# Segment sum of every eighth edge tile as two products of rounded parts, and lane one-hots compared with an iota in PSUM

## The reference

```python
def _L0_gnn_ref(node_features, edge_index, edge_features, mW1, mb1, ...):
    node_i = node_features[i_idx]
    node_j = node_features[j_idx]
    msg_input = jnp.concatenate([node_i, node_j, edge_features], axis=-1)
    h = jax.nn.relu(msg_input @ mW1 + mb1)
    messages = h @ mW2 + mb2
    aggregated = jax.ops.segment_sum(messages, i_idx, num_segments=node_features.shape[0])
    ...
```

## Time and profile before

| | us |
|---|---|
| median of 3 runs | 2928.23 |
| the runs | 2925.83, 2928.23, 2932.85 |
| the profiled execution | 2927.9 |
| its span, first to last instruction | 2926.1 |

### The profile page before, as it was taken

The page is one execution under the profiler, slowest core; times in us unless marked ns, Lnnn a source line. Parts: engine busy times, 40 slices in busy tenths (PEclk is TensorE's granted clock), DMA queues, the critical chain, the costliest instruction groups (busy, mean ns, idle before and its releaser), DMA issues. The chain is left out here.

```text
span 2926.1 us, 34808 instructions
## 1 busy us (share of the span) xinstructions
PE 2337.2 (80%) x8554; PEld 1421.9 (49%) x8554; DVE 1870.9 (64%) x3838; ACT 1030.2 (35%) x2853; POOL 1804.0 (62%) x1842
## 2 busy tenths in 40 slices
PE   5488898229999999998998887888876655556799
PEld 2144443115555555555666664555454433334577
DVE  8897785217777777774544456666645444444898
ACT  1177878217677777662222221000030000000232
POOL 5777777777677676761006566777747777777200
PEclk8799999559999999999999999999778788888899
DMA  9223225029999999996016565555344333333001
GB/s 282 75 62 105 85 87 173 14 65 271 261 270 267 262 266 265 265 264 211 28 56 207 160 200 173 167 169 168 104 124 124 105 106 105 106 105 106 19 1 45
DMA packets 229078, 433.58 MB, mean 148 GB/s; under 512 B 45882, under 2 KB 121292, under 8 KB 228686
## 3 DMA queue, kind: packets, MB, share of 16 engines
q0 software_dynamic: 93888, 248.27, 31.7%
q1 hardware_dynamic: 129504, 177.80, 18.4%
q10 hardware_dynamic: 5488, 5.28, 0.5%
HBM read 310.36 MB, written 122.99 MB: 148 GB/s over the span
## 5 line engine op out<-in xcount | busy, mean ns | idle before, releaser
L958 POOL DMA_INDIRECT qg<-q_d,rb x480 | 479.0, 998 | 207.3 <-issue 103.5
L419 POOL DMA_INDIRECT recs_d<-recs,slot_src x416 | 451.8, 1086 | 146.1 <-issue 132.3
L1909 POOL DMA_INDIRECT nbr_yg<-y_d,gidx x439 | 415.2, 946 | 156.7 <-issue 86.8
L1075 PE MATMUL p_sum<-hb,wide 128*96 128x512 f32 x960 | 451.9, 593 | 1.2 <-ACT hb L1004 1.1
L1004 ACT ACTIVATE hb<-hb 128x512 f32<-128x512 f32 x480 | 297.1, 630 | 205.2 <-DVE hb L1044 201.2
L1748 POOL DMA_INDIRECT nbr_yg<-y_d,gidx x298 | 282.4, 948 | 94.4 <-issue 57.6
L1044 DVE TENSOR_TENSOR hb<-p_h,qg 128x512 f32<-128x512 f32 x480 | 312.6, 680 | 35.3 <-DMA qg<-q_d,rb 31.4
L1349 POOL DMA_INDIRECT n_ahead<-y_d,gidx x141 | 134.8, 956 | 268.8 <-DMA y_d<-n_y 198.5
L443 ACT ACTIVATE lane_hot<-bare_hot,val 128x128 f16<-128x128 f16 x832 | 247.5, 391 | 130.4 <-DVE bare_hot L729 130.1
L1845 PE MATMUL nbr_sum<-nbr_yg,nbr_hot 128*128 128x258 f32 x596 | 215.9, 460 | 67.8 <-DMA nbr_yg<-y_d,gidx 55.8
L1030 DVE SCALAR_TENSOR_TENSOR agg<-agg,keep,p_sum 96x512 f32<-96x512 f32 x240 | 178.1, 742 | 123.3 <-PE p_sum L1075 122.4
(11 more groups left out here) (377 smaller groups left out, 4084.6 us busy)
## 6 DMA issues: line engine op xcount, KB each, us to landing
agg_d<-agg SPq DMA_DIRECT2D x240, 192.4 KB, 5.0
msg_d<-n_ahead SPq DMA_DIRECT2D x141, 128.0 KB, 2.7
nbr_ys<-msg_d SPq DMA_DIRECT2D x141, 128.0 KB, 2.7
nbr_yg<-y_d,gidx POOLq DMA_INDIRECT x737, 2.8
p_low<-p_d SPq DMA_DIRECT2D x11, 768.0 KB, 12.5
recs_d<-fill SPq DMA_DIRECT2D x16, 510.0 KB, 17.5
rb<-recs_d SPq DMA_DIRECT2D x60, 136.0 KB, 5.1
qg<-q_d,rb POOLq DMA_INDIRECT x480, 5.7
```

The source lines that it names most:

```text
L419: pool.indirect_dma_start(S.recs[:, :], bass.IndirectOffsetOnAxis(ap=slot_src[:, c:c + 1], axis=0), recs[:, c, :], None).then_inc(s_scat, 16)
L958: pool.indirect_dma_start(qg[t % QB][:, :], None, S.q[:, :], bass.IndirectOffsetOnAxis(ap=rb[n % RB][:, t % BT, 1:2].bitcast(U32), axis=0) ...
L1075: last = pe.matmul(p_sum[g % 2][0:SB, :], wide[g % XB][:, j, 0:SB], hb[t % HB][:, :], start=(j == 0), stop=(j == 1))
L1909: pool.indirect_dma_start(yg[t % GB][:, 0:D], None, S.y[0:EARLY_NODES, :] if t < NSTORED else S.y[:, :], bass.IndirectOffsetOnAxis(ap=C.gi ...
```

## The change

The lane one-hots: the first 64 numbers of the iota are copied once to `p_iota[:, 440:504]` in PSUM (`lane_row`). Line 729 becomes two instructions, one for each half of the 128 lanes, which add 0 or 64 to `lane_row` and compare with the lane number.

The segment sum: for tiles 0, 8, 16, ... (`is_split`, 60 of 480) ACT writes relu rounded into `h_high` in place of `hb`. A new DVE instruction (`low_part`, behind both additions of the pair) computes max(hb, 0) - h_high into `h_low`. PE multiplies the one-hot part of `wide` with `h_high` and then with `h_low`, both as products of rounded operands, in place of one f32 product. `wide` has the type fp32r now; where it is used in f32 it is only read as such. ACT and DVE wait for the sums of the split tile two before (`s_sum`), PE for `s_h_low`.

The semaphore of the last stage's stores is allocated in `build`.

```diff
@@ sorting_programs
+        lane_row = p_iota[:, NCOL:NCOL + P // 2]
...
             step.link(dve.tensor_copy(iota_c[:, :], lo_i[:, :]))
+            step.link(dve.tensor_copy(lane_row, C.iota_f[:, 0:P // 2]))
...
-            lane_iota = C.iota_f[:, :].rearrange("p (a n) -> p a n", a=1)
+            lane_iota = lane_row.rearrange("p (a n) -> p a n", a=1)
...
-                dve.tensor_tensor(bare_hot[g % BARE][:, :, :], lane_iota.to_broadcast([P, TC, P]),
-                                  lane[:, TC * g:TC * g + TC].rearrange("p (c a) -> p c a", a=1).to_broadcast([P, TC, P]),
-                                  ALU.is_equal).then_inc(s_bare, 1)
+                for half in range(2):
+                    last = dve.scalar_tensor_tensor(
+                        out=bare_hot[g % BARE][:, :, half * P // 2:(half + 1) * P // 2],
+                        in0=lane_iota.to_broadcast([P, TC, P // 2]), scalar=float(half * P // 2),
+                        in1=lane[:, TC * g:TC * g + TC].rearrange("p (c a) -> p c a", a=1).to_broadcast([P, TC, P // 2]),
+                        op0=ALU.add, op1=ALU.is_equal)
+                last.then_inc(s_bare, 1)
@@ stage_sort_and_edges
-        LOAD = 4
+        LOAD, EACH_SPLIT = 4, 4
...
-        wide = [m.sb(f"wide{b}", [P, 2, P]) for b in range(XB)]
+        wide = [m.sb(f"wide{b}", [P, 2, P], F32R) for b in range(XB)]
...
+        h_high = [m.sb(f"h_high{b}", [P, HID], F32R) for b in range(2)]
+        h_low = [m.sb(f"h_low{b}", [P, HID], F32R) for b in range(2)]
...
+        def is_split(t):
+            return t % (2 * EACH_SPLIT) == 0
...
-                        act.activation(hb[t % HB][:, :], hb[t % HB][:, :], ACT.Relu).then_inc(s_relu, 1)
+                        into = hb[t % HB]
+                        if is_split(t):
+                            n = g // EACH_SPLIT
+                            if n >= 2:
+                                act.wait_ge(s_sum, EACH_SPLIT * (n - 2) + 1)
+                            into = h_high[n % 2]
+                        act.activation(into[:, :], hb[t % HB][:, :], ACT.Relu).then_inc(s_relu, 1)
...
+                def low_part(t):
+                    dve.wait_ge(s_relu, t + 1)
+                    n = t // (2 * EACH_SPLIT)
+                    if n >= 2:
+                        dve.wait_ge(s_sum, EACH_SPLIT * (n - 2) + 1)
+                    dve.scalar_tensor_tensor(out=h_low[t // (2 * EACH_SPLIT) % 2][:, :], in0=hb[t % HB][:, :], scalar=0.0,
+                                             in1=h_high[t // (2 * EACH_SPLIT) % 2][:, :].bitcast(F32), op0=ALU.max,
+                                             op1=ALU.subtract).then_inc(s_h_low, 1)
...
+                    if is_split(2 * g):
+                        low_part(2 * g)
...
-                        last = pe.matmul(p_sum[g % 2][0:SB, :], wide[g % XB][:, j, 0:SB], hb[t % HB][:, :],
-                                         start=(j == 0), stop=(j == 1))
+                        if is_split(t):
+                            hot = wide[g % XB][:, j, 0:SB]
+                            pe.matmul(p_sum[g % 2][0:SB, :], hot, h_high[t // (2 * EACH_SPLIT) % 2][:, :], start=(j == 0), stop=False)
+                            pe.wait_ge(s_h_low, t // (2 * EACH_SPLIT) + 1)
+                            last = pe.matmul(p_sum[g % 2][0:SB, :], hot, h_low[t // (2 * EACH_SPLIT) % 2][:, :], start=False, stop=(j == 1))
+                        else:
+                            last = pe.matmul(p_sum[g % 2][0:SB, :], wide[g % XB][:, j, 0:SB].bitcast(F32), hb[t % HB][:, :],
+                                             start=(j == 0), stop=(j == 1))
```

More of the change, by code:

```diff
@@ L899, in stage_sort_and_edges @@
         s_first, s_acc, s_deg = m.sem("e_first"), m.sem("e_acc"), m.sem("e_deg")
+        s_h_low = m.sem("e_h_low")
         recs_v = S.recs[0:NSLOTS, :].rearrange("(n p r) w -> n p r w", p=P, r=BT)
@@ L1053, in transposes @@
                     for j in range(2):
-                        last = pe.transpose(p_tr[g % 2][:, j, :], wide[g % XB][:, j, :], C.ident[:, :])
+                        last = pe.transpose(p_tr[g % 2][:, j, :], wide[g % XB][:, j, :].bitcast(F32), C.ident[:, :])
                     last.then_inc(s_tr, 1)
@@ L2075, in stage_last @@
         s_x3, s_ln, s_weigh, s_sum = (m.sem(n) for n in ("x3", "ln", "weigh", "sum"))
-        s_route, s_dve, s_z, s_out, s_st = (m.sem(n) for n in ("route", "dve", "z", "out_done", "st"))
+        s_route, s_dve, s_z, s_out = (m.sem(n) for n in ("route", "dve", "z", "out_done"))
+        s_st = C.s_out_stored
         FIRST_TURN, FIRST_SPREAD = (0, 3, 10, 19, 22), (6, 8, 13, 15, 17)
@@ L2272, in build @@
         S.msg = dram("msg_d", [NSTORED * P, D])
+        C.s_out_stored = m.sem("out_stored")
         stage_constants(nc, C)
```

## The result

The changed kernel takes 2885.0 us (median of 4 runs, 2879.1 to 2888.6), the kernel before beside it 2930.1: a ratio of 0.9845 with a 95% interval of 0.9824 to 0.9867, so 45 us or 1.5% faster. The forecast was 2871 with a range of 2856 to 2894: right in direction and inside the range, 14 us too hopeful. The number alone does not part it from the rivals: A and D gave 2888, E 2881 to 2891. What parts them is in the traces. The profiled execution took 2885.8 us, its span is 2884.0.

The account below looks back on a forecast made before the run. POOL's 416 scatters were taken to bound the first 640 us and PE the edge stage. Terms: 2927.9 - 41.4 + 0.2 + 0.5 - 16.5 = 2870.7, against the median 2871 us; range 2856 to 2894.

Parts of the forecast that it names:

- A: Rival, edge stage: gathers become its bound, so it gives nothing; 2888 us, chance 0.10.
- D: Rival, edge stage: low part at half rate, 1.22 us, holds POOL 1.06 us, no edge gain; 2888 us, chance 0.03.
- E: Rival, sort stage: scatter gain partly lost waiting for the placing, 10 to 20 us; 2881 to 2891 us, chance 0.05.
- What bounds each stage: First 640 us end with POOL's list of 416 scatters; in the edge stage PE is busy 690.67 of 692 us.
- The hold by two tensors in SBUF: Sort stage: DVE instructions with both tensors in SBUF stretch POOL's scatters; iota in PSUM frees 41.4 us.
- B: Rival, sort stage: new halves hold POOL too, 8 us more stretch, edge saving kept; 2920 us, chance 0.06.
- C: Rival, both stages: every scalar_tensor_tensor holds POOL and gathers bound the edge stage; 2973 us at most, chance 0.02.
- the rule of 0.87 us for each us of DVE work: POOL's hold by DVE instructions with two SBUF tensors; up to 0.6 us for each low part.
- What is late next in the sort stage: Scatters also wait for the placing; these waits were to grow by 0.5 us, 3 us as the worst.
- DVE's cost of the halves: Sort stage: two halves take 1.39 us against 1.22, 9 us on DVE, covered by idle time before the edge stage.
- The split products: Edge stage, 60 split tiles: two rounded products cost PE 0.48 us instead of 0.855; low part 693 ns.
- Their worth: Edge stage: 22.5 us saved on PE, of which 16.5 us was taken as arriving because gathers are late next.

Follow-up runs that it names:

- e3: Changed kernel with the iota of the one-hot halves read from SBUF instead of PSUM; 3311 us (one run) beside 3285 for the kernel before, slower chip.
- e5: Changed kernel with split tiles' sum written back to PSUM, where relu and low part read it; 2877.9 us, ratio 0.9820.
- e1: Kernel before with the change of the lane one-hots alone; 3299.1 us beside 3285.4 on a slower chip, ratio 1.0024.
- e8: Changed kernel with scatters allowed four more groups ahead of the placing (PLACE_LAG 14 instead of 10); 2877.3 us, ratio 0.9817.
- e6: Changed kernel with eight gather buffers (qg) instead of six; 2872.1 us, ratio 0.9805.

## Why the prediction was right or wrong

**What bounds each stage: right where the kernel before takes 2930 us.** POOL's list ended the sort stage and PE's products filled the edge stage; taking from both shortened both.

**The hold by two tensors in SBUF: right in cause and size.** The stretch expected to go was 41.4 us, and POOL's busy time in scatters fell by 41.3. e3 shows that the place of the iota decides whether there is a hold. So B (the halves hold POOL too) and C (every scalar_tensor_tensor does) are out, the latter also by e5's 0.94 us. What the prediction had wrong is the rule of 0.87 us for each us of DVE work, which its rivals B, C and D are priced with: it holds for a scatter that starts with the DVE instruction. One that starts before it is not held, and one that starts late in it is held for the rest alone. The forecast of 41.4 us did not use the rule, it took the whole stretch away. It also gave PSUM all the credit, where on the chip of e1 to e3 a third of it comes from the halving.

**What is late next in the sort stage: the step that failed.** I had 0.5 us for longer waits for the placing, 3 as the worst; it was 2.6 at scatter 76 in the profiled execution, for a reason that I had not added up: the scatters ahead of it came 3 us sooner, while the first lane one-hot started 1 us later in this execution (137.94 against 136.87). With an earlier start, as in e5, this wait is not there, so it belongs to the execution as much as to the change. And 5.9 us went into pauses before every 113th scatter, which I had not seen as pauses: in the earlier trace rows they hide in the "issue" time. These pauses grew in all five executions of the faster scatters outside the slower chips, by 4.5 to 6.7 us in all. Idle time of a list that bounds a stage has to be taken apart by size before the list is made faster, not taken as a mean of 0.3 us. This term was 8 to 9 us too good. The 0.2 us for the copy of the iota can't be seen: the first lane one-hot starts at 136.4 to 137.9 us with the copy, at 136.9 without.

**DVE's cost of the halves: right, on the safe side.** The pair takes 1.28 us, less than two times 0.69, and the idle time before the edge stage covered it.

**The split products: right on PE** (0.47 us for two), on the low part's time (0.69 us, so no halved rate, and D is out) and on its hold (0.5 us of 0.6). **Their worth: mis-sized in the profiled run.** I took 16.5 of 22.5 us; the changed kernel's profile has 7.7, e8's with the same code 17.9. The limit was named (the gather, late next), but I weighed two causes as one. The runs part them: not throughput (e6 at share 0.94 keeps pace), nor, as far as e5 beside e8 shows, POOL's hold, but the number of buffers. The sum of the earlier trace rows could have said it: 0.5 us of pause, 5.7 from issue to landing and 0.7 of addition are 6.9 against a round of 8.4, so the median gather is in time; but the slowest takes 7.5 us to land, and that makes 8.7. So the term of 16.5 us is too good by 9 in the profiled execution, and by nothing in e8; that the 10 us between them are late gathers is seen (82 us of waits against 47), why they were later is not.

Together, in the profiled execution: 41.4 - 0.7 - 32.4 = 8.3 us too much from the sort stage and 16.5 - 7.7 = 8.8 from the edge stage; the stages behind it took 1.9 us less. By the medians the miss is 14 us. Both misses went the same way, and the range held because its upper end had room for A and E; that is the range doing its work and not a sign that the two terms were right.

**E** (scatter gain lost in waits for the placing) holds on the slower chips, where the placing took back 15 us of POOL's 36 and the waits of unshown senders 28. There the rounding behind the placing also ends later than the scatters, which is close to the case that I had named as upsetting the whole. Where the kernel before takes 2930 us, E is the 2.6 us at scatter 76 and no more.

## What to carry to other kernels

If POOL issues indirect DMAs on the path, look at its instructions' durations beside each DVE instruction: two tensors in SBUF stretch those that start while the DVE instruction runs, and moving one constant operand to PSUM takes that away for almost nothing. Cutting the DVE instruction in two takes away a part. Before making a bounding list faster, list its long pauses and its waits one by one, since those may grow by what was gained. When a stage fed by a ring of buffers gets faster, count the round again: here two more buffers took the waits for gathers away, which a cleverer low part did not. And before a gain of 5 us is put down to an edit, run the kernel without it on the same chip: here the same code differed by 10 us in one stage.

## What the runs showed of the hardware

A DVE instruction with two SBUF tensors held a POOL DMA issue that started while it ran until about 0.12 us before its end (2.02 us in place of 0.97 with 1.17 us left); one that started before it was not held (0.96 us with 0.82 us of overlap). With one of the tensors in PSUM there was no hold (0.94 to 0.97 us). Two back-to-back DVE instructions of 0.68 us took 1.28. A product of 512 columns of rounded operands took PE 0.24 us behind others of its kind, an f32 one 0.855. POOL paused 3.0 to 6.6 us before every 113th scatter, the longer in the kernels with faster scatters; the cause is open. And the same kernel took 2930 us on one chip and 3285 to 3329 us on three others, where DVE, ACT and POOL had waits of up to 39 us with no sender shown, the edge stage began behind DVE's work and not behind the last scatter, and PE did not fill it. The change, worth 1.5% where its result was measured, was worth nothing measurable on the one of these three where it ran, 0.15% with an interval that includes none.
